# How the last four heads of each attention get their softmax division

## The reference, cut to what matters

```python
x = x + attn_a(layernorm(x)); x = x + ffn(layernorm(x))
x = x + attn_b(layernorm(x)); x = x + ffn(layernorm(x))
# attention, per head:
w = softmax(q @ k.T / sqrt(16) + mask)      # causal, or a window of 64 keys
a = w @ v                                    # per head 16 values of each query
out = a @ Wp + bp                            # attn_a; attn_b has no bias
```

## Time and profile before

| | |
|---|---|
| three runs | 1640.38, 1645.91, 1649.18 us, median 1645.91 |
| the profiled execution | 1645.49 us, of which the span of its instructions is 1643.6 |
| TensorE (PE) busy | 1374.2 us, 84% |
| VectorE (DVE) busy | 1106.1 us, 67% |
| ScalarE (ACT) busy | 763.0 us, 46% |
| GpSimd (POOL) busy | 403.0 us, 25% |
| mean granted clock of TensorE | 0.924 of full |

### The profile page before, as it was taken

How to read it: one execution, slowest core, us unless ns; L and a number is a source line. 1 busy time by engine, 2 the same in 40 slices (tenths; PEclk the granted TensorE clock), 3 DMA queues, 4 the chain that set the end, 5 groups by cost and what they waited for, 6 DMA issues and landing times.

```text
span 1643.6 us, 24058 instructions
## 1 busy us (share of the span) xinstructions
PE 1374.2 (84%) x9213; PEld 832.9 (51%) x9213; DVE 1106.1 (67%) x1850; ACT 763.0 (46%) x1139; POOL 403.0 (25%) x387
## 2 busy tenths in 40 slices
PE   2698879896899887898888987989797988797968
PEld 2433248554653326754673332765475332485547
DVE  4687566757587736676669764586666875667575
ACT  2326744353335674335442666444443267443533
POOL 1302223211331233212322223320133022232113
PEclk9979989897979998999897999999899799899979
DMA  7610210613060111242324011151414202106130
GB/s 292 192 44 16 92 65 9 171 62 136 28 168 3 60 60 52 65 116 79 118 75 121 15 54 66 40 141 47 140 62 135 49 15 92 65 8 172 62 136 26
DMA packets 87533, 137.66 MB, mean 84 GB/s; under 512 B 24208, under 2 KB 60368, under 8 KB 84048
## 3 DMA queue, kind: packets, MB, share of 16 engines
q1 hardware_dynamic: 87392, 135.71, 27.6%
HBM read 54.07 MB, written 11.61 MB: 40 GB/s over the span
## 4 chain that ended last, share of the span: by engine, by line
PE 54%; DVE 25%; ACT 7%; issue 5%; DMA 5%; POOL 2%; SPq 1%; ACTq 0%; DVEq 0%; another core or an unknown queue 0%; POOLq 0%
DVE peak L621 13%; PE opsum L1097 10%; PE ring L1067 7%; PE ring L1131 6%; PE ring L1044 6%; PE ring L1132 5%; PE opsum L1144 5%; PE ring L1012 4%; ACT probs L859 4%; PE opsum L1145 2%; PE ring L935 2%; DMA on_lo<-osb 2%; DVE rest L602 2%; PE ring L950 1%; DMA on_lo<-onf 1%
## 5 line engine op out<-in xcount | busy, mean ns | idle before, releaser
L859 ACT ACTIVATE probs<-ring 128x768 f32<-128x768 f32 (+5 forms) x496 | 400.6, 836 | 380.9 <-PE ring L1067 253.5
L621 DVE TENSOR_REDUCE peak<-ring 128x4 f32<-128x768 f32 (+7 forms) x480 | 463.6, 1004 | 133.6 <-PE ring L1012 130.5
L1044 PE MATMUL ring<-k_st,q_st 96*128 96x192 bf16 (+4 forms) x1280 | 280.7, 328 | 49.8 <-DVE peak L621 40.4
L1067 PE MATMUL ring<-q_st,k_st 98*128 98x512 bf16 (+5 forms) x1344 | 244.1, 291 | 29.2 <-DVE peak L621 11.5
L1097 PE MATMUL opsum<-probs,V 128*32 128x192 f32 (+5 forms) x2816 | 221.4, 408 | 11.4 <-POOL probs L538 9.5
L1044 PEld LDWEIGHTS ring<-k_st,q_st 96*128 96x128 bf16 x1280 | 101.6, 103 | 173.1 <-DVE peak L621 92.1
L1067 PEld LDWEIGHTS ring<-q_st,k_st 98*128 98x128 bf16 x1344 | 91.8, 97 | 185.4 <-ACT probs L859 67.1
L547 POOL TENSOR_TENSOR h_lo<-hid,h_hi 128x512 fp32r<-128x512 f32 x96 | 124.0, 1295 | 228.5 <-ACT h_hi L893 228.5
L538 POOL TENSOR_SCALAR_AFFINE_SELECT probs<-probs 128x512 f32<-128x512 f32 x128 | 81.6, 637 | 393.9 <-ACT probs L859 393.9
L1131 PE MATMUL ring<-xt_hi,w_gu_sb 128*128 128x512 f32 x384 | 157.3, 410 | 19.6 <-DVE xt_lo L578 12.5
L1012 PE MATMUL ring<-mask_a,ident_b 128*128 128x128 bf16 (+2 forms) x704 | 162.3, 284 | 0.0
(11 more groups left out here) (115 smaller groups left out, 1973.7 us busy)
## 6 DMA issues: line engine op xcount, KB each, us to landing
w_gu_sb<-img_gu SPq DMA_DIRECT2D x16, 1536.0 KB, 6.8
w_qkv<-img_qkv SPq DMA_DIRECT2D x9, 1536.0 KB, 7.6
q_st<-q_part SPq DMA_DIRECT2D x96, 128.0 KB, 2.4
q_st<-q_part SPq DMA_DIRECT2D x48, 256.0 KB, 4.8
on_hi<-o_hi SPq DMA_DIRECT2D x64, 128.0 KB, 2.7
k_st<-k_part SPq DMA_DIRECT2D x48, 144.0 KB, 2.5
k_st<-k_part SPq DMA_DIRECT2D x24, 288.0 KB, 7.2
k_st<-k_part SPq DMA_DIRECT2D x48, 128.0 KB, 2.4
```

The lines of the kernel that those rows point to most:

```text
L621: dve.tensor_reduce(peak[:, g % 2, :].rearrange("p (h i) -> p h i", i=NT)[:, h:h + heads, i], heads_of(plan.slot[e], unit, plan.a_width(i) ...
L859: act.activation(probs[:, j % 2, h:h + heads, 0:w], heads_of(plan.slot[e], unit, w), ACT.Exp).then_inc(exp_done, 1)
L1044: pe.matmul(flat(plan.slot[e])[:, per * n + c:per * n + c + d], q, k_st[0:SP_ROWS, HG * g + h0 + n, first_key + c:first_key + c + d], star ...
L1067: last = pe.matmul(flat(plan.slot[e])[:, per * n + c:per * n + c + d], kk, q_st[:, HG * g + h0 + n, q0 + c:q0 + c + d], start=(per * n % 5 ...
```

## The change

For the last group the events C, R and M take D's place. ScalarE copies the bank to `osb`; its sums go out by transfer; the reciprocal is taken of 16 columns; it comes back by transfer; shuffle and product follow. The result stands in `onf` for this group too. `direct` goes, and the counts that the waits use are raised from six C and R per attention to eight.

```diff
-                        later.append((pe + 0.2, ("C" if g < GROUPS - 1 else "D", g, self.last.index(k))))
+                        later.append((pe + 0.2, ("C", g, self.last.index(k))))
...
-                elif kind == "D":
-                    dve = max(dve, at) + 4.6
-                    later.append((dve + 0.1, ("H", g, k)))
...
-COPIED, NORMED = 2 * GROUPS - 2, 2 * GROUPS
+NORMED = 2 * GROUPS
...
                     elif kind == "R":
-                        dve.wait_ge(sums_out[k], 16 * ((GROUPS - 1) * a + g + 1))
+                        dve.wait_ge(sums_out[k], 16 * (GROUPS * a + g + 1))
                         dve.reciprocal(rsum[:, k, :], sums[:, k, :]).then_inc(rsum_done, 1)
                     elif kind == "M":
-                        dve.wait_ge(rsum_back[k], 16 * ((GROUPS - 1) * a + g + 1))
+                        dve.wait_ge(rsum_back[k], 16 * (GROUPS * a + g + 1))
                         dve.stream_shuffle(onf[:, k, :], onf[:, k, :], [0] * 32).then_inc(bcast_done, 1)
...
-                    elif kind == "D":
-
-                        dve.wait_ge(pv_done, V_BASE[a] + plan.n_j * g + plan.last[k] + 1)
-
-                        dve.wait_ge(on_f, NORMED * a + plan.nth["M", g - 1, k] + 1)
-                        dve.stream_shuffle(osb[:, k, :], opsum[:, k, :], [1] * 32).then_inc(bcast_done, 1)
-                        dve.wait_ge(bcast_done, NORMED * a + plan.nth[e] + 1)
-                        dve.reciprocal(osb[:, k, :], osb[:, k, :]).then_inc(direct, 1)
-                        dve.wait_ge(direct, 2 * a + k + 1)
-                        dve.tensor_tensor(osb[:, k, :], opsum[:, k, :], osb[:, k, :], ALU.mult).then_inc(on_f, 1)
...
-                        mult = ("D" if g == GROUPS - 1 else "M", g, k)
-                        act.wait_ge(on_f, NORMED * a + plan.nth[mult] + 1)
+                        act.wait_ge(on_f, NORMED * a + plan.nth["M", g, k] + 1)
                         if 4 * a + g:
                             act.wait_ge(packed[k], 32 * (4 * a + g))
-                        act.activation(o_hi[:, k, :], normed(g)[:, k, :], ACT.Copy).then_inc(on_hi_done, 1)
+                        act.activation(o_hi[:, k, :], onf[:, k, :], ACT.Copy).then_inc(on_hi_done, 1)
```

More of the change, by code:

```diff
@@ L82, in __init__ @@
         self.ring = [e for e in self.events if e[0] in "QATB"]
-        kinds = ["MD" if e[0] in "MD" else e[0] for e in self.events]
+        kinds = [e[0] for e in self.events]
         self.nth = {e: kinds[:n].count(kinds[n]) for n, e in enumerate(self.events)}
@@ L378, in layers_kernel @@
                   "turned xhi_done xlo_done qk_ready qk_evac part_hi part_rest part_mid part_lo stack0 stack1 stack2 "
-                  "v_ready v_half v_done masked direct a_ready a_max t_ready peak_hi peak_done peak_rows "
+                  "v_ready v_half v_done masked a_ready a_max t_ready peak_hi peak_done peak_rows "
                   "b_ready exp_done pv_done o_copied sums_out0 sums_out1 rsum_done rsum_back0 rsum_back1 "
@@ L385, in layers_kernel @@
          turned, xhi_done, xlo_done, qk_ready, qk_evac, part_hi, part_rest, part_mid, part_lo, stack0, stack1, stack2,
-         v_ready, v_half, v_done, masked, direct, a_ready, a_max, t_ready, peak_hi, peak_done, peak_rows,
+         v_ready, v_half, v_done, masked, a_ready, a_max, t_ready, peak_hi, peak_done, peak_rows,
          b_ready, exp_done, pv_done, o_copied, sums_out0, sums_out1, rsum_done, rsum_back0, rsum_back1,
@@ L400, in layers_kernel @@
             stack0: 2 * 192, stack1: 2 * 192, stack2: 2 * 192, v_ready: sum(VT), v_half: sum(VT) + 1, v_done: sum(VT),
-            masked: V_BASE[1], direct: 4,
+            masked: V_BASE[1],
             a_ready: A_ALL, a_max: A_ALL, t_ready: 8, peak_hi: 8, peak_done: 8, peak_rows: 8 * 32,
             b_ready: B_ALL, exp_done: B_ALL, pv_done: V_ALL,
-            o_copied: 12, sums_out0: 96, sums_out1: 96, rsum_done: 12, rsum_back0: 96, rsum_back1: 96,
+            o_copied: 16, sums_out0: 128, sums_out1: 128, rsum_done: 16, rsum_back0: 128, rsum_back1: 128,
             bcast_done: 16, on_f: 16, on_hi_done: 16, on_lo_done: 16, packed0: 256, packed1: 256, x_bias: 2,
@@ L457, in proj_bank @@
             return (ring[:, 2, 0, :], ring[:, 2, 1, :], opsum[:, 0, :])[t % 3]
-        def normed(g):
-            return osb if g == GROUPS - 1 else onf
         def cols(h):
@@ L529, in _ @@
                             pool.wait_ge(on_hi_done, NORMED * a + plan.nth[e] + 1)
-                            o = normed(g)[:, k, :]
+                            o = onf[:, k, :]
                             pool.tensor_tensor(o.bitcast(F32R), o, o_hi[:, k, :].bitcast(F32),
@@ L1093, in attention @@
                             if opens and g > 0:
-                                pe.wait_ge(o_copied, COPIED * a + 2 * (g - 1) + bank + 1)
+                                pe.wait_ge(o_copied, NORMED * a + 2 * (g - 1) + bank + 1)
                             for h in range(HG):
@@ L1320, in attention @@
                     elif kind == "C":
-                        sp.wait_ge(o_copied, COPIED * a + plan.nth[e] + 1)
+                        sp.wait_ge(o_copied, NORMED * a + plan.nth[e] + 1)
                         sp.dma_start(sums[:, k, :], osb[1:P:32, k, :]).then_inc(sums_out[k], 16)
                     elif kind == "R":
-                        sp.wait_ge(rsum_done, COPIED * a + plan.nth[e] + 1)
+                        sp.wait_ge(rsum_done, NORMED * a + plan.nth[e] + 1)
                         if 4 * a + g:
@@ L1333, in attention @@
                         c = slice(HALF * k, HALF * k + HALF)
-                        for dst, src in ((on_hi, o_hi), (on_lo, normed(g))):
+                        for dst, src in ((on_hi, o_hi), (on_lo, onf)):
                             sp.dma_start(dst[rows, g // 2, c].bitcast(F32),
```

## The result

The changed kernel took 1666.3 us (median of four runs, 1664.4 to 1667.8), the kernel before 1646.7 (four runs): ratio 1.0124, 95% interval 1.0093 to 1.0156. It is slower. Beside the later experiments, on one chip with six more runs of the changed kernel and 23 of before, the ratio was 1.0098 (1.0074 to 1.0123): 16 us, or 18 by the medians. The profiled execution spans 1662.5 us, against 1643.6.

What follows compares the result with a forecast made beforehand. No engine fills the span, so it took what ends last at each attention's tail, eight in all, as the bound. 1645.5 + 4 x (2.8 + 2.3) = 1665.9 us, range 1654 to 1674.

Steps and rivals of the forecast that it cites:

- The transfers, 1.91 and 1.81: In both tails: sums out take 1.91 us from issue to the waiting reciprocal, reciprocals back 1.81 us.
- The copy behind B18, product at 221.91: Causal tail: ScalarE's copy of bank 0 waits behind an exp; product ends at 221.91, 2.4 us late.
- K0 behind R1 on SyncE, 0.4: Causal tail: bank 0's copies queue behind the issue of bank 1's reciprocals, 0.4 us more delay.
- Causal tail 2.8 us: Projection 0 starts 2.8 us late in each causal tail, passed on whole to the gate-up matmuls.
- R0 and R1 held on SyncE until the copies of group 2 land: Windowed tail: reciprocals' return transfers wait for the previous group's copies; projection 0 is 3.1 us late.
- The event order worked: Both tails: the planner puts the copy where VectorE's direct division stood, with nothing before that point moving.
- Windowed tail 2.3 us: xt_lo comes 1.8 us late and gate-up starts at half clock, so its seventeenth matmul is 2.3 us late.
- at half clock after 2.4 us of waiting: Windowed gate-up start: TensorE runs cold after this wait, as in the causal row; warm would cost 1.8 us.
- Rival C: Both tails: small transfers cost 2.84 us each, 2.0 more per tail, giving 1681.7 us; chance 0.11.
- Rival D: Whole attention: the planner settles on another lead, reordering score and exp work; 15 us either way allowed; chance 0.05.
- The chance of 0.90 on slower: Whole kernel: slower by more than about 0.5%, 8 us; faster got 0.03 and within 0.07.

Runs made afterwards that it cites:

- the copy without transfers: The kernel before, but in the causal tail ScalarE copies the bank to SBUF and VectorE divides all 512 columns there: ratio 1.0039, 6.4 us.
- the two halves: Transfers only in the causal attention's last group, or only in the windowed one's, each against the kernel before: 1.0063 (10.4 us) and 1.0040 (6.6 us).
- control: The kernel before run once more with nothing changed: ratio 0.9997, profile of 1650.9 us.
- its own high part: The kernel before with a separate high-part tile for the last group, so that step skips waiting for group 2's copies: 0.9972, 4.6 us faster.

## Why the prediction was right

The forecast was 1665.9 us and the median 1666.3. The mechanism was right in both tails; that the number was hit so closely is in part luck, since one term was too large (below). Its steps, against the first batch's timelines (shifted as above to the times of the trace of before):

- *The transfers, 1.91 and 1.81.* 1.90 and 1.85. The Trainium skill's fixed cost of about 2.0 us (DMA: Bandwidth & Descriptors, Anatomy of one DMA) is a little over both; the rows decide.
- *The copy behind B18, product at 221.91.* 215.78, and 221.86. Shown apart by the copy without transfers.
- *K0 behind R1 on SyncE, 0.4.* 0.35 in the timeline, 0.32 when the order was turned round.
- *Causal tail 2.8 us.* The tail grew by 2.18 in the mean and the last P·V was 0.59 later (I had 0.6): 2.8, 11.1 in four batches; 10.4 measured alone.
- *R0 and R1 held on SyncE until the copies of group 2 land.* R0 at 380.23 (forecast 380.2), product 383.51 (383.45), projection 0 at 388.91 (388.85), xt_lo at 401.15 (401.15), gate-up at 402.90 (402.75). The event order worked was the one that ran.
- *Windowed tail 2.3 us: this term was too large.* In the first batch it was right: the seventeenth gate-up matmul came at 409.03, 2.5 after the old one. The other batches gave less. In the mean the tail grew by 0.76, the last P·V by 0.43, and the stretch to the seventeenth matmul by 0.52 (5.51 to 6.03): 1.7 us, 6.8 in four batches instead of 9.2, and 6.6 measured alone. I had taken the first batch for all. There the old gate-up ran at full clock at once (4.83 us); in the others it took 5.19, 5.89 and 6.14, and in the last two the granted clock was 0.77 and 0.72 in the first 6.2 us, so the old tail was often at half clock as well. That a start is at half clock after 2.4 us of waiting and at full clock after 1.50 was taken from two rows, and more rows contradict it: in the profile with transfers in the causal tail only, a gate-up start after 2.79 us of waiting had a granted clock of 1.00, and one after 1.59 us had 0.74. That stretch also moved in the causal tail, for which the forecast had nothing: 6.25 to 5.75 us in the mean of the first two profiles, 5.87 to 6.13 in the second pair. It has no sure sign and is left out of the 2.8.

So the tails give 17.9 us, the two halves 17.0, side by side the whole 16, and the first comparison 19.6, which hit the forecast of 20.4 more closely than the sum deserved. The difference lies within the intervals. Rival C (dearer hops) is ruled out by the 1.85 and 1.90. Rival D (another lead in the planner, so another order of the score and exp work) did not happen: all 9213 matmuls and all 496 exps come in the same order in both traces. The chance of 0.90 on slower was borne out.

## What to carry to other kernels

Work that is cheap on its engine can be dear as latency: two small transfers and a copy cost 1.2 us more than the long reciprocal that they saved, though VectorE's load fell by 51 us. In the causal tail VectorE had nothing else to do, so its time there counted as latency only. When a chain is moved to other engines, look at what stands before it in each queue: in the causal tail the copy with its place on ScalarE cost 1.3 us, and the transfers 0.6 beyond the reciprocal that they replaced. And before a calculation is made cheaper, look at whether the buffer that it fills is free; one more tile of 4 KB per partition gained 4.6 us, where the change lost 16.

## What the runs showed of the hardware that I had not expected

TensorE's half-clock stretches do not end at the same place in the same work. In the second batch's causal attention the granted clock fell to half 10 to 11 us after the first score matmul, in two executions of the same work, the kernel before and its control (columns as in rows 7):

```profile
478.00:498.40 20.40, 19.94 (x75) 7.81 (x74) 20.37 (x24) 0.00 (x0) 0.05 (x1) 0.50 0.52 125
498.50:502.00 3.50, 2.65 (x17) 0.99 (x16) 3.32 (x5) 1.23 (x2) 0.00 (x0) 1.00 0.01 2
```

```profile
480.90:508.10 27.20, 26.60 (x97) 10.47 (x96) 25.49 (x30) 3.07 (x3) 0.00 (x0) 0.50 0.35 80
508.20:512.00 3.80, 3.49 (x26) 1.30 (x28) 3.19 (x4) 2.75 (x3) 0.64 (x1) 1.00 0.00 0
```

TensorE's matmuls fill 19.94 of 20.40 us, and 26.60 of 27.20, and the granted clock is still half, 1.2 of 2.4 GHz, all through: for 20 us in one execution and 27 in the other. VectorE is busy nearly all the time as well (20.37 and 25.49 us), so not all that the clock costs TensorE need show in the total. The three later causal attentions, from their first score matmul to the last P·V, took 149.3 us each in the first profile of before and 150.8, 150.2 and 150.2 in the control. In the changed kernel they took 150.7, 151.5 and 151.5 in the first profile and 153.1, 152.9 and 149.8 in the second, of which 0.5 is the copy's displacement. The profiles of before and of its control differ by 7.3 us at a mean granted clock of 0.924 and 0.916, and 3.4 of it lies in these three attentions. So part of every comparison of totals above comes from such stretches.

GpSimd's subtraction of bank 0's high part took 1.76 to 1.77 us in all four windowed tails of the kernel before with its own high part, where it runs beside VectorE's product of two SBUF tiles, against 1.27 elsewhere. No run here tests the cause.
